# Attention B of a four-layer hybrid kernel: value products stream 128 columns instead of 96, the mask product contracts 128 rows instead of 88

## The chip, the cores and the metric

The kernel runs on one core of one Trainium2 chip, as one launch. The metric is the device time of that core in microseconds (us), the median over runs. Inside the core there are five engines with queues of their own: TensorE (PE for the matmul, PEld for the load of its stationary operand), VectorE (DVE), ScalarE (ACT), GpSimd (POOL) and SyncE (SP, which only issues transfers here). They wait for each other by semaphores.

## The reference, cut to what matters

The input `x` is (32, 256, 128) in f32. Four residual layers follow each other; the third is the one that the change touches:

```python
x = x + attn_a(layernorm(x))
x = x + ffn(layernorm(x))
x = x + attn_b(layernorm(x))
x = x + ffn(layernorm(x))

# attn_b: 16 heads of width 8, T = 256 tokens in 4 segments of 64
for each segment (q, k, v):
    A_mem = (sigma(q) @ M) / (sigma(q) . z + eps)      # memory of the segments before
    scores = where(causal, -inf, q @ k.T / sqrt(8))
    A_dot = softmax(scores) @ v                        # inside the segment
    A = beta * A_mem + (1 - beta) * A_dot
    M, z = M + sigma(k).T @ (v - V_prev), z + sum(sigma(k))
out = A @ W_o.T
```

## The kernel before

The program is three blocks one after the other: `attention_a` (to about 920 us of the trace), `dense` (the second half of attention A's block and the first feed-forward, to about 1150 us), and `attention_b` (from about 1150 us to the end; it also holds the last feed-forward, folded into one matrix for each pair of batch elements).

`attention_b` runs over 32 batch elements as a software pipeline: in step `n`, each engine does the input and projections of element `n`, scores and memory of element `n - 1`, softmax and value products of elements `n - 1` and `n - 2`, and the output of element `n - 3`. A step has `ST = 8` stages `s`, and the order within a stage is written out by hand for each engine. The first steps are peeled, the middle is a loop over pairs of steps. No planner orders anything: each engine executes its list and waits where the list says.

What PE does in each stage, in this order (all in the function for `block.tensor`):

- **The mask product and the transposed scores, L1507 and L1512.** One bf16 matmul puts minus the row maximum and the causal mask into `t_ps` for two heads: its moving operand is `late` (rows 0 to 63: the mask; rows 64 to 87: the row maxima in three bf16 parts for eight heads), its stationary operand is `pick`, which selects from them. Both tiles have `BROWS = 64 + 24 = 88` rows. Eight small products (64 x 64, in pairs) add the scores. ACT takes the exponential into `prob` (L1424).
- **The value product, L1558.** For the two heads of pair `g` (`before(lag, g)` names them) and each half `t` of the tokens, `prob` (128 x 128, f32) is the stationary operand, and `WIN = 96` columns of `vb`, from `at = g * VP` on, stream through. `VP = 36` columns belong to the pair; the columns behind them fall where the next pairs write later, so what they write is overwritten. The profile counts two passes of PE for each f32 matmul: 8 pairs x 2 halves x 2 passes = 32 passes of L1558 for an element, 1024 in all. When all eight pairs are done, DVE normalizes (L1838 to L1842), and PE may start on `o_ps` of the next element only then (`ad_d`).
- Between them stand, at their stages: the scores for the row maxima (L1529, L1533), the recurrence over the segments (L1486, L1493, with DVE between them), the transposes (L1545, L1569, L1572, L1581, L1588, L1623), the projections (L1603, L1604 with 256 columns; L1609, eight passes of 128 columns), the output product (L1595, 128 columns) and the folded feed-forward (L1632, 128 columns).

`VW = VP * 7 + WIN` is the width of `vb`. POOL fills `vb` with zeros once (L1307), writes ones beside the values (L1310), and then writes the values of each element (L1334). DVE fills the rows 64 to 127 of `k_st` and `q_st` with zeros in step 0 (`stack_zeros`, L1642 and L1643), and builds rows 64 to 87 of `pick` there (`picks`, L1649 to L1653); ACT copies the masks into rows 0 to 63 of `pick` and `late` (L1403, L1404) and, for each element and half of the heads, the row maxima into rows 64 to 87 of `late` (L1460).

The lines on which the change turns:

```python
WIN = 96
VW = VP * (H // 2 - 1) + WIN
BROWS = SEG + NPART * H // 2
pick, late = sb("pick", [BROWS, H // 4, 2, SEG], BF16), two("late", [BROWS, T], BF16)
...
pe.matmul(t_ps, pick[:, g % (ST // 2), :, :].rearrange("p a k -> p (a k)"),
          late[g // (ST // 2)][:, :], start=True, stop=True)
...
mm = pe.matmul(o_ps[:, t, at:at + WIN], prob[g % 4][:, t * P:(t + 1) * P],
               vb[st][:, t, at:at + WIN], start=True, stop=True)
```

Of the kernel before, what the change touches and what calls it, by code (L numbers as in the profile page):

```python
# [13 lines left out]
F32 = mybir.dt.float32  # L14
BF16 = mybir.dt.bfloat16
# [4 lines left out]
P = 128  # L20
NB, T = 32, 256
NT = T // P
H, HD, R, QK = 16, 8, 8, 32
# [1057 lines left out]
def attention_b(nc, d):  # L1081

    ctx = ExitStack()
    with ctx:
        sb, sem = memory(nc, ctx, "c")
        SEG = 64
# [2 lines left out]
        MW = HV + H  # L1089
        VP = 2 * 2 * (HD + 1)  # L1090

        WIN = 96
        VW = VP * (H // 2 - 1) + WIN
        BROWS = SEG + NPART * H // 2
        ST = 8
# [5 lines left out]
        w_o = sb("w_o", [P, P])  # L1101
        ident, ident16 = sb("ident", [P, P]), sb("ident16", [P, P], BF16)
        causal = sb("causal", [P, 512], BF16)
        pick, late = sb("pick", [BROWS, H // 4, 2, SEG], BF16), two("late", [BROWS, T], BF16)
        pick8 = sb("pick8", [P, H // 2])
        causal32 = sb("causal32", [P, P + SEG])
        diag = sb("diag", [P, MW])
# [34 lines left out]
        spare, loaded, loaded_late = sem("spare"), sem("loaded"), sem("loaded_late")  # L1142
        const_d, beta_d = sem("const_d"), sem("beta_d")
        mask_d, pick_d = sem("mask_d"), sem("pick_d")
        zeros_d = [sem(f"zeros_d{i}") for i in range(2)]

        x_in, xt_in, wc_in = sem("x_in"), sem("xt_in"), sem("wc_in")

# [240 lines left out]
        @block.scalar  # L1389
        def _(act):  # L1390
            act.wait_ge(loaded, N_LOAD * 16)
            act.copy(ident16[:, :], ident[:, :]).then_inc(mask_d, 1)

            def masks():

                act.wait_ge(loaded_late, N_LATE * 16)
                for k in range(2):
                    ks = slice(k * SEG, (k + 1) * SEG)
                    act.copy(causal[ks, :].rearrange("p (c f) -> p c f", c=H // 2),
                             causal32[ks, ks].unsqueeze(1).broadcast_to([SEG, H // 2, SEG])).then_inc(mask_d, 1)  # L1400
                for k in range(2):
                    act.copy(late[k][0:SEG, :].rearrange("p (c f) -> p c f", c=NS),
                             causal32[0:SEG, P:].unsqueeze(1).broadcast_to([SEG, NS, SEG])).then_inc(mask_d, 1)  # L1403
                act.copy(pick[0:SEG, :, :, :].rearrange("p g a k -> p (g a) k"),  # L1404
                         ident[0:SEG, 0:SEG].unsqueeze(1).broadcast_to([SEG, H // 2, SEG])).then_inc(mask_d, 1)
                act.activation(bexp[:, :], beta[:, 0:1], ACT.Exp, scale=-1.0).then_inc(beta_d, 1)

            def body(j, u):
                n, i = 2 * j + u, u
                for s in range(ST):  # L1410
                    if s == 1 and active(j, u, 1):
                        b = n - 1
                        act.wait_ge(sk_p, b + 1)
                        if later(j, b, 1):
                            act.wait_ge(mem_p, b * 3)
                        act.copy(skn[0:SEG, :, :].rearrange("p s f -> p (s f)"),
                                 ps_c[0:SEG, 0:(NS - 1) * P]).then_inc(sk_d, 1)
                    lag, g = turn(s)
                    if active(j, u, lag):
                        b = n - lag  # L1420
                        act.wait_ge(shifted, b * ST + g + 1)
                        if g >= 4 or later(j, b, 1):
                            act.wait_ge(pv, b * ST + g - 3)
                        act.activation(prob[g % 4][:, :], t_ps, ACT.Exp).then_inc(exped, 1)  # L1424
                    if s == 0 and active(j, u, 3):
                        b = n - 3
                        act.wait_ge(at_p, b + 1)
                        if isinstance(b, int) and b == 0:
                            act.wait_ge(beta_d, 4)
                        if later(j, b, 1):  # L1430
                            act.wait_ge(wo_p, b)
                        act.activation(at_b[:, :], ps_a[:, 0:T], ACT.Copy, scale=beta[:, 3:4]).then_inc(at_d, 1)
                    if s == 0 and active(j, u, 0):
                        act.wait_ge(zt_p, n + 1)
                        act.copy(zt[i][:, :, :, :], ps_b[:, 0:T].rearrange("p (s t) -> p s t", s=NS).unsqueeze(2)
                                 .broadcast_to([P, NS, 2, SEG])).then_inc(zt_d, 1)
                    if s == 1 and active(j, u, 0):
                        act.wait_ge(kq_p, n + 1)
                        act.copy(kq[i][:, 0, :], ps_a[:, 0:T]).then_inc(kq_d, 1)
                        act.mul(kq[i][:, 1, :], ps_a[:, T:2 * T], HD ** -0.5).then_inc(kq_d, 1)  # L1440
                    if s == 3 and active(j, u, 0):
                        act.wait_ge(vs_p, n + 1)
                        if later(j, n, 2):
                            act.wait_ge(mem_p, (n - 1) * 3)
                        else:
                            act.wait_ge(const_d, 9 + 7 * n)
                        act.copy(uv[i][0:SEG, :, 0:HV], ps_b[0:SEG, 0:(NS - 1) * P].rearrange("p (s f) -> p s f", f=P)
                                 ).then_inc(vs_d, 1)
                        if later(j, n, 1):
                            act.wait_ge(v_d, n * VD)  # L1450
                        act.copy(vs[:, :, :].rearrange("p s f -> p (s f)"), ps_b[:, :]).then_inc(vs_d, 1)
                        act.wait_ge(pn_d, (n + 1) * 2)
                        if later(j, n, 1):
                            act.wait_ge(sg_d, n)
                        act.activation(nexp[:, :, :], neg[:, :, :], ACT.Exp).then_inc(nexp_d, 1)
                    for h2 in range(2):
                        if s == MT_AT[h2] and active(j, u, 1):
                            b = n - 1
                            act.wait_ge(mt_p, 2 * b + h2 + 1)
                            act.copy(late[h2][SEG:BROWS, :], mt_ps).then_inc(mt_d, 1)  # L1460
                    if s == 5 and active(j, u, 3):
                        b = n - 3
                        act.wait_ge(z4_p, b + 1)
                        act.copy(z4t[:, :], ps_b[:, 0:T]).then_inc(z4t_d, 1)
                if isinstance(j, int) and n == 0:
                    masks()

            pipeline(act, body, ahead=1)

        @block.tensor  # L1470
        def _(pe):
            pe.wait_ge(loaded, N_LOAD * 16)

            def body(j, u):
                n, i = 2 * j + u, u
# [20 lines left out]
                for s in range(ST):  # L1496
                    lag, g = turn(s)
                    if active(j, u, lag):

                        b, st = n - lag, (i + lag) % 2  # L1500
                        if isinstance(b, int) and b == 0 and g == 0:
                            pe.wait_ge(pick_d, 3)
                        if g % (ST // 2) == 0:
                            pe.wait_ge(mt_d, 2 * b + g // (ST // 2) + 1)
                        if g >= 1 or later(j, b, 1):
                            pe.wait_ge(exped, b * ST + g)
                        pe.matmul(t_ps, pick[:, g % (ST // 2), :, :].rearrange("p a k -> p (a k)"),  # L1507
                                  late[g // (ST // 2)][:, :], start=True, stop=True)
                        for c in range(NS):
                            cs = slice(c * SEG, (c + 1) * SEG)  # L1510
                            for hh in range(2):
                                mm = pe.matmul(t_ps[hh * SEG:(hh + 1) * SEG, cs],  # L1512
                                               k_st[st][:, 2 * g + hh, cs], q_st[st][:, 2 * g + hh, cs],
                                               start=False, stop=True, skip_group_check=True)
                        mm.then_inc(shifted, 1)
# [123 lines left out]
        def _(dve):  # L1639
            def stack_zeros(i):  # L1640

                dve.memset(k_st[i][SEG:P, :, :].bitcast(F32), 0.0).then_inc(zeros_d[i], 1)  # L1642
                dve.memset(q_st[i][SEG:P, :, :].bitcast(F32), 0.0).then_inc(zeros_d[i], 1)  # L1643

            def picks():

                at = lambda a: ident[SEG:BROWS, SEG + a * H // 2:SEG + (a + 1) * H // 2]
                eight = pick8[SEG:BROWS, :]
                dve.tensor_tensor(eight, at(0), at(1), ALU.add).then_inc(pick_d, 1)  # L1649
                dve.wait_ge(pick_d, 1)  # L1650
                dve.tensor_tensor(eight, eight, at(2), ALU.add).then_inc(pick_d, 1)
                dve.wait_ge(pick_d, 2)
                dve.tensor_copy(pick[SEG:BROWS, :, :, :].rearrange("p g a k -> p (g a) k"),  # L1653
                                eight.unsqueeze(2).broadcast_to([BROWS - SEG, H // 2, SEG])).then_inc(pick_d, 1)

# [271 lines left out]
```

## Time and profile before

| | us |
|---|---|
| median of 3 runs | 2051.97 |
| lowest and highest | 2045.56, 2061.51 |
| the profiled execution, its own time | 2052.87 |
| its span in the trace | 2050.7 |
| PE busy | 1686.4 (82%) |
| PEld busy | 1405.3 (69%) |
| DVE busy | 1417.8 (69%) |
| POOL busy | 841.3 (41%) |
| ACT busy | 772.2 (38%) |
| mean granted clock of PE | 0.849 |

The profile is one execution of the program. Busy shares are means over three blocks with different limits, so they say little about one of them. The granted clock is the share of full speed at which PE's array was clocked: it has two levels, 1.00 (2.4 GHz) and 0.50 (1.2 GHz), and a figure between them is a mean over a stretch in which both occurred. The same matmul takes about twice as long at the lower level, and counts as busy all that time. So a stretch that shows more busy time of PE need not hold more work.

### The profile page before, as it was taken

The page shows a single profiled execution, that of the slowest core. Times are in us where ns is not written, and L with a number is a line of the kernel's source. Part 1 is how long each engine was busy: PE and PEld are TensorE (multiplying, and loading weights), DVE is VectorE, ACT ScalarE, POOL GpSimd, SP SyncE. Part 2 cuts the span into 40 slices and gives each one's busy share as a digit, 9 for nine tenths or more (in the row PEclk, how much of TensorE's full clock was granted, in tenths as well). Part 3 has the DMA queues.
Part 4 walks back from the last instruction along what each step waited for, and adds up shares of the span by engine and source line. Part 5 has one row for each costly group of instructions (what it writes and reads, how often), then busy time and mean ns, then how long its engine had stood idle before and what let it go on. Part 6 is the DMA issues. An engine that isn't in the chain of part 4 may idle for free. (4 is left out here: it accounts for less than half of the span.)

```text
span 2050.7 us, 47252 instructions
## 1 busy us (share of the span) xinstructions
PE 1686.4 (82%) x14500; PEld 1405.3 (69%) x14564; DVE 1417.8 (69%) x3490; ACT 772.2 (38%) x1666; POOL 841.3 (41%) x1052
## 2 busy tenths in 40 slices
PE   5999999999999999994666378888888888888887
PEld 3888888888888888893555356666666666666665
DVE  5578888888888888875888555655565555555653
ACT  1455555555555555561222222222222222222221
POOL 3445455444454554534556323333333333323330
PEclk9999999999999999996998667877787777777775
DMA  3322222222211222213332122222222222222220
GB/s 115 122 73 81 74 73 72 74 77 72 72 69 69 72 75 71 75 40 95 96 92 82 55 87 81 88 79 74 73 82 77 80 80 80 76 82 80 77 80 17
DMA packets 178621, 158.10 MB, mean 77 GB/s; under 512 B 9457, under 2 KB 160113, under 8 KB 178546
## 3 DMA queue, kind: packets, MB, share of 16 engines
q1 hardware_dynamic: 178546, 157.16, 23.2%
q8 instruction: 40, 0.66, 0.1%
q14 instruction: 35, 0.29, 0.1%
HBM read 113.09 MB, written 44.04 MB: 77 GB/s over the span
## 5 line engine op out<-in xcount | busy, mean ns | idle before, releaser
L600 PE MATMUL a_bank<-a_vp,a_prob 128*128 128x96 f32 x4096 | 544.5, 277 | 0.3 <-ACT a_prob L457 0.3
L600 PEld LDWEIGHTS a_bank<-a_vp,a_prob 128*128 128x128 f32 x4096 | 511.0, 196 | 17.0 <-ACT a_prob L457 8.7
L633 DVE TENSOR_REDUCE a_nmax<-a_bank 128x2 f32<-128x512 f32 x512 | 331.3, 686 | 122.1 <-PE a_bank L527 121.7
L457 ACT ACTIVATE a_prob<-a_bank 128x512 f32<-128x512 f32 x512 | 306.1, 598 | 179.2 <-PE a_bank L582 170.3
L1558 PE MATMUL c_o_bank<-c_vb,c_prob 128*128 128x96 f32 x1024 | 218.7, 351 | 37.4 <-DVE c_ad L1842 36.4
L1558 PEld LDWEIGHTS c_o_bank<-c_vb,c_prob 128*128 128x128 f32 x1024 | 185.5, 253 | 51.4 <-DVE c_ad L1842 34.6
L527 PE MATMUL a_bank<-a_k_st,a_q_st 96*128 96x256 bf16 x1024 | 206.4, 285 | 8.4 <-DVE a_nmax L633 6.2
L582 PE MATMUL a_bank<-a_q_st,a_k_st 120*128 120x256 bf16 x1024 | 201.8, 279 | 0.0
L1424 ACT ACTIVATE c_prob<-c_bank 128x256 f32<-128x256 f32 x256 | 98.4, 385 | 232.6 <-PE c_bank L1512 229.4
L335 POOL TENSOR_TENSOR a_prod<-a_ov,a_wgt 128x2048 f32<-128x2048 f32 x32 | 119.1, 3721 | 144.5 <-DVE a_wgt L706 131.8
L466 ACT COPY a_ov<-a_bank 128x292 f32<-128x292 f32 x256 | 103.0, 403 | 114.0 <-PE a_bank L600 114.0
L364 POOL TENSOR_SCALAR a_q_st<-a_mt 24x2048 bf16<-24x2048 bf16 x64 | 122.3, 1911 | 39.8 <-PE a_bank L582 23.8
L1352 POOL TENSOR_SCALAR c_parts<-c_kq 128x512 bf16<-128x512 f32 x32 | 19.9, 621 | 282.9 <-ACT c_kq L1440 282.9
L1334 POOL TENSOR_SCALAR c_vb<-c_vs 64x128 f32<-64x128 f32 x128 | 39.8, 311 | 224.0 <-PE c_o_bank L1558 173.6
L735 DVE TENSOR_REDUCE a_ao<-a_prod 128x128 f32<-128x1024 f32 x64 | 126.0, 2011 | 7.7 <-POOL a_prod L335 7.7
L527 PEld LDWEIGHTS a_bank<-a_k_st,a_q_st 96*128 96x128 bf16 x1024 | 102.7, 107 | 32.3 <-DVE a_nmax L633 15.3
L1512 PEld LDWEIGHTS c_bank<-c_q_st,c_k_st 128*64 128x64 bf16 x2048 | 61.2, 126 | 74.0 <-issue 67.1
L582 PEld LDWEIGHTS a_bank<-a_q_st,a_k_st 120*128 120x128 bf16 x1024 | 100.5, 107 | 15.3 <-issue 0.4
L1533 PE MATMUL c_bank<-c_k_st,c_q_st 128*64 128x64 bf16 x2048 | 66.9, 217 | 35.4 <-issue 21.2
L1493 PE MATMUL c_bank<-c_mz,c_sg 128*128 128x144 f32 x192 | 60.4, 404 | 42.1 <-DVE c_mz L1727 42.1
L1711 DVE TENSOR_REDUCE c_nmax<-c_bank 128x8 f32<-128x512 f32 x128 | 85.8, 679 | 10.2 <-PE c_bank L1533 9.9
L1512 PE MATMUL c_bank<-c_q_st,c_k_st 128*64 128x64 bf16 x2048 | 92.0, 220 | 0.0
(198 smaller groups left out, 3073.0 us busy)
## 6 DMA issues: line engine op xcount, KB each, us to landing
a_q_st<-scratch_a_parts_dram SPq DMA_DIRECT2D x192, 96.0 KB
a_k_st<-scratch_a_parts_dram SPq DMA_DIRECT2D x64, 288.0 KB
c_q_st<-scratch_c_parts_dram SPq DMA_DIRECT2D x192, 96.0 KB
c_k_st<-scratch_c_parts_dram SPq DMA_DIRECT2D x64, 288.0 KB
scratch_a_parts_dram<-a_parts SPq DMA_DIRECT2D x32, 384.0 KB, 2.7
scratch_c_parts_dram<-c_parts SPq DMA_DIRECT2D x32, 384.0 KB, 2.7
a_x<-in_x SPq DMA_DIRECT2D x32, 128.0 KB, 10.6
scratch_y<-a_y SPq DMA_DIRECT2D x32, 128.0 KB, 9.3
```

Of the source, the lines that this page charges most:

```text
L335: pool.tensor_tensor(prod[:, :, :].rearrange("p g (r e) -> p g r e", r=R), ov[o][:, :, 0:RD].rearrange("p g (r e) -> p g r e", r=R), wgt[: ...
L364: pool.tensor_scalar(q_st[o][MROW:AROWS, hs, :], mt[half_][MROW:AROWS, :].unsqueeze(1).broadcast_to([AROWS - MROW, H // 2, T]), 1.0, 0.0, ...
L457: act.activation(prob[h % 4][:, :, :].rearrange("p a b -> p (a b)"), t_ps[h % 2][:, :], ACT.Exp).then_inc(exped, 1)
L466: act.copy(ov[(i + lag) % 2][:, 4 * g:4 * g + 4, :], o_ps[g % 2][:, 0:4 * VC].rearrange("p (g c) -> p g c", g=4)[:, :, 0:CQ]).then_inc(ov_ ...
L527: mm = pe.matmul(s_ps[t][:, hh * T:(hh + 1) * T], q_st[o][0:MROW, 2 * g + hh, t * P:(t + 1) * P], k_st[o][0:MROW, 2 * g + hh, :], start=Tr ...
L582: mm = pe.matmul(t_ps[h % 2][:, c * T:(c + 1) * T], k_st[o][0:AROWS, h, c * P:(c + 1) * P], q_st[o][0:AROWS, h, :], start=True, stop=True)
L600: mm = pe.matmul(o_ps[g % 2][:, at:at + VC], prob[h % 4][:, c, t * P:(t + 1) * P], vp[o][:, c, :], start=c == 0, stop=c == NT - 1)
L633: dve.tensor_reduce(nmax[:, t, 2 * g:2 * g + 2], s_ps[t][:, :].rearrange("p (h k) -> p h k", h=2), AX.X, ALU.max, negate=True).then_inc(ma ...
L735: dve.tensor_reduce(ao[o][:, t, :].rearrange("p (h e) -> p h e", h=H), prod[:, :, :].rearrange("p (h i) (r e) -> p i h e r", i=NT, r=R)[:, t],
L1424: act.activation(prob[g % 4][:, :], t_ps, ACT.Exp).then_inc(exped, 1)
L1512: mm = pe.matmul(t_ps[hh * SEG:(hh + 1) * SEG, cs], k_st[st][:, 2 * g + hh, cs], q_st[st][:, 2 * g + hh, cs], start=False, stop=True, skip ...
L1558: mm = pe.matmul(o_ps[:, t, at:at + WIN], prob[g % 4][:, t * P:(t + 1) * P], vb[st][:, t, at:at + WIN], start=True, stop=True)
```

## The change

The value product streams 128 columns of `vb` instead of 96. `vb` grows by 32 columns for each half (`VW` from 348 to 380), which stay zero or hold values of later pairs; the result's extra columns lie in `o_ps` up to column 380 of 512 and are overwritten or not read.

`pick` and `late` get 128 rows instead of 88, and the mask product contracts all of them. Rows 88 to 127 are set to zero once: DVE gets a memset for each of the two `late` tiles (beside the two of `stack_zeros`) and one for `pick`, with a step more in the chain of `pick_d`; ACT waits for the memset of `late` (`late_d`) before its first two copies into it. The number of matmuls, their order, and all other waits stay.

```diff
-        WIN = 96
+        WIN = 128
...
-        pick, late = sb("pick", [BROWS, H // 4, 2, SEG], BF16), two("late", [BROWS, T], BF16)
+        pick, late = sb("pick", [P, H // 4, 2, SEG], BF16), two("late", [P, T], BF16)
...
-        zeros_d = [sem(f"zeros_d{i}") for i in range(2)]
+        zeros_d, late_d = [sem(f"zeros_d{i}") for i in range(2)], sem("late_d")
...
                             b = n - 1
+                            if isinstance(b, int) and b == 0:
+                                act.wait_ge(late_d, h2 + 1)
                             act.wait_ge(mt_p, 2 * b + h2 + 1)
...
-                            pe.wait_ge(pick_d, 3)
+                            pe.wait_ge(pick_d, 4)
...
                 dve.memset(q_st[i][SEG:P, :, :].bitcast(F32), 0.0).then_inc(zeros_d[i], 1)
+                dve.memset(late[i][SEG:P, :].bitcast(F32), 0.0).then_inc(late_d, 1)
...
             def picks():
 
+                dve.memset(pick[SEG:P, :, :, :].rearrange("p g a k -> p (g a k)").bitcast(F32), 0.0
+                           ).then_inc(pick_d, 1)
+                dve.wait_ge(pick_d, 1)
```

## Rows read from the trace of the kernel before

**Rows 1.** The page: span, busy time of each engine, and granted clock by slice.
```profile
span 2050.7 us, 47252 instructions
...
PE 1686.4 (82%) x14500; PEld 1405.3 (69%) x14564; DVE 1417.8 (69%) x3490; ACT 772.2 (38%) x1666; POOL 841.3 (41%) x1052
...
PEclk9999999999999999996998667877787777777775
```

**Rows 2.** Windows, attention A: bounds, length, busy of each engine, PEclk, DMA, GB/s.
```profile
50.00:900.00 850.00, 775.50 (x6440) 706.54 (x6439) 699.79 (x1332) 452.77 (x924) 414.44 (x424) 0.96 0.22 76
```

**Rows 3.** Windows, 24 periods of attention B, L1609 to L1609: some, and the sum.
```profile
1474.51:1501.95 27.44, 22.90 (x219) 17.41 (x220) 15.92 (x52) 7.55 (x19) 8.52 (x15) 0.75 0.22 76
1501.95:1526.43 24.48, 19.89 (x218) 14.91 (x220) 15.40 (x52) 7.51 (x19) 8.77 (x15) 0.86 0.26 86
...
1580.88:1608.99 28.11, 23.69 (x219) 18.17 (x221) 15.98 (x52) 7.54 (x19) 8.52 (x15) 0.70 0.22 75
1608.99:1634.29 25.30, 20.95 (x219) 15.81 (x222) 15.66 (x53) 7.53 (x19) 9.02 (x15) 0.80 0.25 83
...
1740.23:1769.07 28.84, 25.05 (x220) 18.93 (x220) 15.27 (x52) 7.54 (x19) 8.39 (x15) 0.64 0.21 73
...
sum 641.22, PE 533.94 PEld 405.35 DVE 375.29 ACT 180.34 POOL 208.02; mean PE 22.25 PEld 16.89 DVE 15.64 ACT 7.51 POOL 8.67
```

**Rows 4.** Windows around two falls of the clock in attention B.
```profile
1512.30:1515.70 3.40, 1.61 (x18) 1.15 (x17) 3.10 (x13) 0.75 (x2) 1.28 (x4) 0.99 0.31 102
1515.70:1522.50 6.80, 6.33 (x45) 4.46 (x44) 1.49 (x4) 1.78 (x5) 0.00 (x0) 0.50 0.35 121
...
1584.00:1587.40 3.40, 1.58 (x20) 1.08 (x16) 2.66 (x7) 0.54 (x2) 2.57 (x4) 0.99 0.14 31
1587.40:1604.40 17.00, 15.57 (x116) 12.26 (x117) 8.03 (x28) 3.79 (x10) 1.22 (x4) 0.50 0.28 99
```

**Rows 5.** Timeline of PE, clock 0.50: start, us, line, tiles, shapes, count.
```profile
1590.63 1.17 PE L1558 MATMUL c_o_bank<-c_vb,c_prob 128*128 128x96 f32 x4
1591.59 1.11 PE L1632 MATMUL c_bank<-c_wc,c_z4t 128*128 128x128 f32 x4
1592.49 0.42 PE L1507 MATMUL c_bank<-c_late,c_pick 88*128 88x256 bf16 x1
...
1603.36 1.11 PE L1603 MATMUL c_bank<-c_zt,c_w_kq 128*128 128x256 f32 x2
```

**Rows 6.** Timeline of PE, the same two kinds of product at clock 1.00.
```profile
1509.77 0.69 PE L1558 MATMUL c_o_bank<-c_vb,c_prob 128*128 128x96 f32 x4
1510.29 0.64 PE L1632 MATMUL c_bank<-c_wc,c_z4t 128*128 128x128 f32 x4
1510.76 0.27 PE L1507 MATMUL c_bank<-c_late,c_pick 88*128 88x256 bf16 x1
```

**Rows 7.** Single lines over the whole trace: count, duration ns min/median/max, first and last start.
```profile
L1507 PEld LDWEIGHTS c_bank<-c_late,c_pick x256: 95/116/211, 1193.6 to 2032.7; 88*128 88x128 bf16 x128
L1529 PEld LDWEIGHTS c_bank<-c_causal,c_ident x128: 95/98/152, 1181.2 to 2011.9; 128*128 128x128 bf16 x128
```

**Rows 8.** Groups by line and form, 1200 to 2000 us: count, busy, mean ns.
```profile
L1558 PE MATMUL c_o_bank<-c_vb,c_prob 128*128 128x96 f32 x960 | 201.3, 346 | 35.7 <-DVE c_ad L1842 34.7 <-POOL c_vb L1334 1.0
...
L1507 PE MATMUL c_bank<-c_late,c_pick 88*128 88x256 bf16 x240 | 80.6, 336 | 0.0
```

**Rows 9.** Chain that ended last, 1500 to 1560 us: start, us, what.
```profile
1519.82 0.80 PE c_o_bank L1558 x4
1520.62 0.91 PE c_bank L1603 x2
...
1524.15 1.16 POOL c_rest L1353
```

**Rows 10.** Timeline of DVE in the first steps of attention B.
```profile
1161.88 1.76 DVE L1643 MEMSET c_q_st<- 64x2048 f32 x1 [0.37 <-issue]
...
1170.36 0.63 DVE L1680 TENSOR_SCALAR c_z<-c_x,c_mv,c_rs 128x128 f32<-128x128 f32 x2 [4.69 <-POOL c_rs L1321]
...
1183.16 0.31 DVE L1722 TENSOR_TENSOR c_mz<-c_bank,c_diag 128x144 f32<-128x144 f32 x1 [5.52 <-PE c_bank L1486]
```

**Rows 11.** Single line: POOL's memset of `vb`.
```profile
L1307 POOL MEMSET c_vb<- x2: 683/683/683, 1159.4 to 1171.1; 128x696 f32 x2
```

More of the change, by code:

```diff
@@ L1649, in picks @@
                 dve.tensor_tensor(eight, at(0), at(1), ALU.add).then_inc(pick_d, 1)
-                dve.wait_ge(pick_d, 1)
+                dve.wait_ge(pick_d, 2)
                 dve.tensor_tensor(eight, eight, at(2), ALU.add).then_inc(pick_d, 1)
-                dve.wait_ge(pick_d, 2)
+                dve.wait_ge(pick_d, 3)
                 dve.tensor_copy(pick[SEG:BROWS, :, :, :].rearrange("p g a k -> p (g a) k"),
```

## The prediction

> **What bounds the kernel now.** I read the page first. PE is busy 82% of the span, and its clock is near full in the first half and lower in the last [rows 1]. The change touches attention B alone, so I compared the blocks by windows: attention A runs at a mean clock of 0.96 [rows 2], and 24 consecutive periods of attention B (from one start of the value projection L1609 to the next, one batch element each) at 0.76. They sum to 641.22 us, or 26.72 us a period, with PE busy 22.25 us of it [rows 3]. DVE, the next engine, is busy 15.64 us. Attention B is PE's, with parts of each period in which PE waits for others.
>
> Then I looked at the periods one by one, since the same work is done in each. They don't take the same time: 24.48 us at a clock of 0.86, 25.30 at 0.80, 27.44 at 0.75, 28.11 at 0.70, 28.84 at 0.64 [rows 3]. Of the 24, seven lie at 0.86, four at 0.80, three at 0.75 to 0.76, nine at 0.70 and one at 0.64. The number of instructions is equal, and so, within half a microsecond, is what DVE does. So the clock sets the period: from 0.70 to 0.86 is worth 28.11 - 24.48 = 3.63 us. That is the price list for everything below.
>
> Next: what goes before a fall and a rise. Twice the clock fell to 1.2 GHz behind a stretch in which PE was busy less than half the time: 1.61 of 3.40 us, and 1.58 of 3.40 us [rows 4]. That is the place where PE waits for DVE (the recurrence, and the normalization before the next value products: 34.7 us in all behind L1842 [rows 8]). The rise is the odd part. In one period the clock stayed low for 6.8 us, in the next for 17.0 us, though PE was busy 15.57 us of these 17.0, or 92% [rows 4]. So "busy" is not what brings it back. What ran there was value products of 96 columns, mask products of 88 rows and pairs of 64-column products; it rose when the wide projections L1603 and L1604 (256 columns, 128 rows) had run, the first of them at 1603.36, one microsecond before the stretch ended [rows 5].
>
> **The change, part by part.**
>
> *Value products, direct cost.* 1024 passes stream 32 columns more. The trace has both widths side by side. At 1.2 GHz four passes of 96 columns take from 1590.63 to 1591.59, 0.96 us, and the four passes of 128 columns behind them from there to 1592.49, 0.90 us [rows 5]. At 2.4 GHz the same two take 0.52 and 0.47 us [rows 6]. The wider one is not slower in either: every f32 pass loads 128 stationary columns, and this load, which both have, sets the pace. I take 0. Bounds: none below 0; above, if the pass were paced by its columns, the pitch of 0.130 us would grow by a third, 0.043 us, at 2.4 GHz (0.240 and 0.080 at 1.2 GHz), which is 1024 x 0.043 = 44 us to 1024 x 0.080 = 82 us. The rows stand against that.
>
> The Trainium skill ("TensorE: Matmul & The Clock Gate", section "Back-to-back issue gap") has a rule that speaks against the change: the gap between matmuls is the streamed columns over the clock plus a small constant. By it 32 columns more are an estimated 13.3 ns a pass at 2.4 GHz, or 14 us for 1024 passes, and the sum below would come out 14 us higher. This trace does not agree: four passes of 128 columns take no longer than four of 96, 0.47 against 0.52 us.
>
> *Value products, tail.* The result of the last pass comes up to 32 columns later, once an element where DVE waits for it; a fourth of a pass's 0.130 to 0.240 us is 0.03 to 0.06, times 32 elements 1 to 2 us at most. I take 0 and leave 2 us in the range.
>
> *Mask product.* 256 products contract 40 rows more. Its load of 88 rows takes at least 95 ns, that of the causal product with 128 rows at least 95 ns as well, medians 116 and 98 [rows 7]: rows cost nothing. I take 0. If the busy time of 336 ns a product [rows 8] grew as the rows do, by 45%, it would be 256 x 0.15 = 39 us; nothing in the rows points there.
>
> *Start.* The memset of 64 x 2048 f32 takes 1.76 us [rows 10]. The two of `late` (64 x 128) and the one of `pick` (64 x 256) are a sixteenth and an eighth of it, 0.11 and 0.22 us, say 0.3 each with their starts, 0.9 us in all. The first `late` and all behind it in DVE's queue come ahead of waits of 4.69 us for POOL and of 5.52 us for PE [rows 10], which hide them; if the cover were gone it would be 0.9 us once. POOL's memset of `vb` grows from 696 to 760 columns, 683 ns by a tenth, twice [rows 11]: 0.1 us. ACT's two new waits are for memsets long past when its first copies come; nothing queues behind them. Value 0, bounds 0 and 1 us.
>
> *The clock.* What is left is whether fuller products bring the clock back sooner. Every stage has one group of four value passes and one mask product. The value passes put a third more columns through the array without taking longer, and the mask product uses all 128 rows instead of 88. In the 17.0 us stretch that is nearly all of what ran between the narrow score products. The fall behind the idle gap stays: the change puts no work into it. So no period should do better than those that already fall and recover fast, 24.48 us at 0.86. The lower bound of the effect is none: each period as it is.
>
> Between them I choose by the periods. The eleven at 0.80 or above have short low stretches and I leave them. The thirteen at 0.76 or below sum to 365.3 us, 28.10 each; they hold stretches like that of 17.0 us, busy and low, and these I let come down to the 25.30 us of a period at 0.80. That is 13 x (28.10 - 25.30) = 36.4 us over 24 periods, 1.52 us each; attention B has 31 periods between its 32 elements, so 31 x 1.52 = 47 us. It lies on the path: in the low stretch the chain of waits goes through the value products and projections one behind the other, and then through POOL's split, which the clock doesn't shorten [rows 9]; the period rows have this in them already, since they are whole periods.
>
> **The sum.** 0 + 0 + 0 - 47 = -47 us against the profiled execution's 2052.87 us (span 2050.7 and 2.2 around it): 2005.9. The median of the runs lies 0.9 lower, at 2051.97, so I forecast 2005.
>
> **The rivals.**
>
> 1. *The clock doesn't follow the width.* For it: attention A uses value products of the same 96 columns and holds 0.96 [rows 2]; its PE is busy 775.5 of 850 us, and maybe gaps alone decide. Against it: 15.57 busy us of 17.0 at 1.2 GHz [rows 4]. The time is then that of before, 2052 (with the start, 2053).
>    The Trainium skill (same page, section "Why this matters for your kernels") advises keeping TensorE busy without long idle gaps, and names no width. By that rule this change does nothing to the clock, as in this rival. The trace agrees for the falls, which stand behind gaps, and not for the 17.0 us.
> 2. *All periods recover at once.* Every period goes to 24.48: 31 x (26.72 - 24.48) = 69 us, so 1983. For it: all periods hold the same work, and only thirteen of 24 are in the long form. Against it: even the short ones split, seven at 0.86 and four at 0.80, so a mixture is what equal work settles in. If the falls went too, the same price of 3.63 us for 0.16 would give 0.14 x 22.7 = 3.2 us a period more and 1884; PE's waits for DVE are not touched, so I give it almost nothing.
> 3. *Slower: the extra columns set the pace.* Place: the 1024 passes of L1558. The load and the stream may be balanced such that 128 columns fit only where the neighbours are of the same kind. Price 0.043 to 0.080 us a pass, 44 to 82 us; without a gain of the clock 2096 or more. It decides from 47 / 1024 = 0.046 us a pass on: there it eats the forecast gain. Against it: [rows 5, 6].
>
> **How the numbers follow.** Forecast (half to most of the long low stretches go, 1990 to 2030): 0.47. Rival 2 and better (below 1990): 0.20. Rival 1, with a gain too small to see (2032 to 2056): 0.27. Rival 3: 0.06. The range reaches from a little below rival 2, 1972, to just past the kernel as it is, 2054; it holds about 0.85, and the likeliest case's own range is 1990 to 2030. One per cent, 20.5 us, is about what a measurement of this kernel can tell from no change (its three runs spread over 16 us). Faster by over 1%, below 2031: 0.67. Within 1%: 0.27. Slower: 0.06.
>
> **What would show it.** In the changed kernel's profile: the mean clock of attention B's periods near 0.82 instead of 0.76; periods at 0.70 with 28 us rare, those at 0.80 and 0.86 with 24.5 to 25.3 us common; four passes of L1558 still 0.5 us apart at 2.4 GHz and 0.9 to 1.0 at 1.2; L1507 at 88 and 128 rows alike; attention A unchanged at 0.96. Rival 1 is shown by an equal split of period lengths, rival 3 by a pitch of L1558 at 2.4 GHz of 0.17 us. The forecast is wrong if the clock stays low through busy stretches of full-width products, or if the periods grow shorter by less than the price list says because POOL's or DVE's part of the chain takes over.

## The result and the profile after

The changed kernel takes 1995.56 us (median of 4 runs, 1986.52 to 2002.17) against 2048.76 us of the kernel before (4 runs, 2042.15 to 2061.51): 53 us less, ratio 0.973 with a 95% interval of 0.9666 to 0.9794. The profiled execution is the shortest of its four (1986.52 us), so its trace shows somewhat more gain than the medians do: spans of 2050.7 and 1984.6 us, 66 us apart. Below, times of whole kernels are medians, and times of parts come from the traces. Two runs of the variants below, one with 64 columns (2160.99 us) and one with less than half of the added work (1955.85 us), fell in a slower state of the chip and are left out of the medians.

The page of the changed kernel, against [rows 1]: span, busy time of each engine, and granted clock by slice of the span.

```profile
span 1984.6 us, 47321 instructions
...
PE 1630.1 (82%) x14564; PEld 1344.4 (68%) x14564; DVE 1418.8 (71%) x3493; ACT 771.1 (39%) x1666; POOL 839.4 (42%) x1052
...
PEclk9999999999999999997898968988888888888887
```

DVE, ACT and POOL are as busy as before to within 2 us. PE streams more columns and is busy 56 us less. The clock row has mostly 8 where it had 7 in attention B; ahead of it the mean clock is the same in both traces, 0.96 from 50 to 900 us and 0.85 from 900 to 1150 us.

Windows of the changed kernel: 24 consecutive periods of attention B, then two of them, to be held against [rows 3] (columns: bounds, length, busy time of PE, PEld, DVE, ACT, POOL with counts, granted clock, DMA share, GB/s).

```profile
1299.98:1899.74 599.76, 499.62 (x5280) 365.23 (x5281) 376.51 (x1225) 179.71 (x456) 206.92 (x337) 0.85 0.25 84
...
1521.93:1547.94 26.01, 22.12 (x220) 15.95 (x220) 15.47 (x52) 7.50 (x19) 8.70 (x15) 0.80 0.24 81
...
1649.96:1673.65 23.69, 19.19 (x220) 14.34 (x220) 15.94 (x52) 7.40 (x19) 8.53 (x15) 0.93 0.26 89
```

The sum is 599.76 us where it was 641.22: 24.99 us a period in place of 26.72, at a mean clock of 0.85 in place of 0.76. Of the 24 periods, 13 lie at 0.86, seven at 0.80 and four at 0.93. Not one is at 0.76 or below, where thirteen were. The price list still holds: 24.3 to 25.1 us at 0.86 (24.4 to 25.2 before), 25.8 to 26.0 at 0.80 (25.3 to 26.2 before), 23.7 at 0.93.

The falls themselves stayed. Counted in the two traces over the 24 periods, the clock falls to 1.2 GHz 37 times before and 39 times after. What changed is how long it stays there: 303.8 us in all before, 174.1 after. Before, twelve of the stretches at 1.2 GHz lasted 10 to 20 us; after, none lasts more than 6.8 us, and 27 of the 39 are over after 3.4 us, like this one of the period at 0.93:

```profile
1656.46:1659.88 3.42, 3.42 (x35) 2.81 (x34) 2.42 (x9) 0.65 (x3) 0.00 (x0) 0.50 0.18 75
```

Where the 66 us of the two spans come from: 2.7 us ahead of the first period (start of the first L1609 at 1162.6 and of the same product, now L1611, at 1159.9 us), 52 us in the 31 periods, and 11 us behind the last of them, which the next rows show, before and after:

```profile
1978.97:2050.70 71.73, 56.25 (x440) 42.96 (x441) 29.54 (x100) 13.62 (x34) 9.59 (x18) 0.55 0.12 38
```

```profile
1924.10:1984.60 60.50, 44.04 (x441) 32.65 (x441) 29.59 (x101) 13.56 (x34) 9.98 (x18) 0.77 0.14 45
```

The pipeline drains there with the same 440 matmuls, at a clock of 0.55 before and 0.77 after. Part of these 11 us may be chance: the trace of the kernel that differs from the one before in attention A alone (128 columns there, below) has the same drain at a clock of 0.71, in 63.4 us.

A fall of the clock in the changed kernel, as in [rows 4]: PE waits (3.04 us busy of 4.80), the clock falls, and it rises again after 6.8 us.

```profile
1682.60:1687.40 4.80, 3.04 (x34) 2.24 (x33) 3.99 (x16) 1.13 (x3) 1.25 (x4) 0.98 0.29 95
1687.40:1694.20 6.80, 6.80 (x46) 4.66 (x44) 1.49 (x4) 1.69 (x4) 0.00 (x0) 0.51 0.35 119
```

### The profile page after: what moved, and what is told of

Its sections match the earlier page's. It is cut to its first block and busy times, and to the rows that moved or that the text cites. A ratio compares the mean times of both kernels' runs of the same rounds, so it can differ in the third digit from the quotient of the medians.

```text
span 1984.6 us, 47321 instructions
## 1 busy us (share of the span) xinstructions
PE 1630.1 (82%) x14564; PEld 1344.4 (68%) x14564; DVE 1418.8 (71%) x3493; ACT 771.1 (39%) x1666; POOL 839.4 (42%) x1052
## 5 line engine op out<-in xcount | busy, mean ns | idle before, releaser
L1560 PE MATMUL c_o_bank<-c_vb,c_prob 128*128 128x128 f32 x1024 | 198.5, 323 | 39.3 <-DVE c_ad L1848 39.3
L1560 PEld LDWEIGHTS c_o_bank<-c_vb,c_prob 128*128 128x128 f32 x1024 | 158.8, 220 | 52.2 <-DVE c_ad L1848 35.0
L1514 PEld LDWEIGHTS c_bank<-c_q_st,c_k_st 128*64 128x64 bf16 x2048 | 56.5, 118 | 64.0 <-issue 56.2
L1495 PE MATMUL c_bank<-c_mz,c_sg 128*128 128x144 f32 x192 | 50.0, 342 | 44.5 <-DVE c_mz L1733 44.5
L1514 PE MATMUL c_bank<-c_q_st,c_k_st 128*64 128x64 bf16 x2048 | 86.2, 210 | 0.0
L1509 PE MATMUL c_bank<-c_late,c_pick 128*128 128x256 bf16 x256 | 78.8, 308 | 0.0
```

The source lines that it names most:

```text
L1514: mm = pe.matmul(t_ps[hh * SEG:(hh + 1) * SEG, cs], k_st[st][:, 2 * g + hh, cs], q_st[st][:, 2 * g + hh, cs], start=False, stop=True, skip ...
```

## The experiments

Theory W: the wider value products bring the clock back sooner, and do nothing else. Its rivals: the 128 rows of the mask product do it; the wider products help PE by themselves; it is chance in how the periods meet the falls. Beside it theory F: the falls come from the gaps in which PE waits for DVE.

### Each half alone

128 columns, 88 rows:

```diff
-        WIN = 96
+        WIN = 128
```

> The value products stream 128 columns, the mask product keeps 88 rows. Theory W (the columns of the value products bring the clock back sooner): most of the change's gain of 53 us is here, 35 to 50 us off the kernel before, mean clock of attention B's periods 0.83 to 0.86 against 0.76. Rival R (it is the 128 rows of the mask product): within 10 us of the kernel before, clock 0.76 to 0.78. Rival S (the phase in which the clock's falls meet the periods shifted, by chance): anything between, and not in step with the width.

Measured: 1996.91 us, ratio to before 0.973 (0.9657 to 0.9804). The whole gain, within 2 us of the full change, and 3 us more than the 50 that I had expected at most. Its 24 periods:

```profile
1310.24:1911.06 600.82, 500.89 (x5280) 366.41 (x5281) 375.60 (x1225) 179.77 (x456) 206.85 (x337) 0.85 0.25 84
```

96 columns, 128 rows (the changed kernel with one line back):

```diff
-        WIN = 128
+        WIN = 96
```

> The mask product contracts 128 rows, the value products keep 96 columns. Theory W: 0 to 18 us faster than before, since these are 8 matmuls of about 45 in each period and gain 40 rows of 128. Rival R: 35 to 53 us faster. If both e1 and this one give the whole gain, either is enough to cross what the clock wants; if neither does, it needs both.

Measured: 2024.42 us (2007.01 to 2032.29), ratio 0.9826 (0.9737 to 0.9916). Faster than the kernel before by more than the expected 18 us: 26 us by the medians, 36 by the ratio of runs. The periods:

```profile
1318.01:1942.56 624.55, 533.41 (x5281) 394.75 (x5281) 372.43 (x1225) 180.18 (x456) 207.79 (x337) 0.79 0.24 81
```

They are 0.70 us shorter each. All 31 periods of this trace, which is of the slowest of its four runs, are 18 us shorter than those before (798.4 and 816.4 us), just within what I had expected. So rows count too, though how much is less certain than for the columns; the two halves don't add: 53 and 26 us alone, 53 together. The columns are sufficient, and on top of them the rows bring nothing that can be measured.

### The width as a dose

The kernel before with fewer columns, and the changed kernel with more:

```diff
-        WIN = 96
+        WIN = 64
```

> The kernel before with 64 columns in place of 96. Theory W, other direction: the clock stays low longer, mean 0.65 to 0.72 in attention B, 20 to 60 us slower than before although less is streamed. Rival C (streamed columns cost time and nothing else): not slower; each group of four passes ends 32 columns earlier, 27 to 53 ns, so up to 10 us faster.

```diff
-        WIN = 128
+        WIN = 160
```

> The changed kernel with 160 columns in place of 128. Up to 128 columns the load of the weights paces a pass (112 ns at 2.4 GHz, 213 at 1.2 in both traces); beyond it the columns do: 32 more are 64 cycles a pass, 27 to 53 ns, 1024 passes, 28 to 55 us of PE time. Theory W: the clock rises further, to 0.88 to 0.92 in attention B, which gives back 10 to 25 us; sum 5 to 30 us slower than the changed kernel. If the pace were still the load's, it would be 10 to 25 us faster than the changed kernel.

```diff
-        WIN = 128
+        WIN = 192
```

> The changed kernel with 192 columns. With 160 the pitch of a pass was 136 ns at 2.4 GHz and 267 at 1.2 (the columns pace it), and still the clock (0.91 in attention B) gave back more than that cost. 192 should take 160 and 320 ns a pass, 1024 x 24 = 25 us more at 2.4 GHz. Theory W: the clock can gain at most 0.09 more, worth 10 to 20 us at 2 us a period for 0.09, so 0 to 20 us slower than with 160 columns; the best width is near 160. If each further column paid for itself, it would be faster than 1980.

| columns | median, us | ratio to before (95%) | clock of the 24 periods | their mean length, us |
|---|---|---|---|---|
| 64 (88 rows) | 2132.72 | 1.0366 (1.0265 to 1.0466) | 0.56 | 29.51 |
| 96 (before, 88 rows) | 2050.15 | 1 | 0.76 | 26.72 |
| 128 (88 rows) | 1996.91 | 0.973 (0.9657 to 0.9804) | 0.85 | 25.03 |
| 160 (128 rows) | 1979.91 | 0.963 (0.9558 to 0.9703) | 0.91 | 24.42 |
| 192 (128 rows) | 1979.15 | 0.9658 (0.96 to 0.9716) | 0.92 | 24.57 |

The clock follows the width over the whole range, so it isn't chance. (Between 128 and 160 the rows change too; at 128 columns they brought nothing that could be measured.) With 64 columns, less work, the kernel is 83 us slower, at a clock of 0.56; I had expected at most 60, and 0.65 to 0.72. Its 24 periods, and a stretch of 42 us in them:

```profile
1319.78:2028.05 708.27, 671.35 (x5280) 497.50 (x5281) 359.09 (x1232) 181.00 (x456) 206.18 (x339) 0.56 0.21 71
...
1480.00:1522.00 42.00, 40.12 (x295) 29.58 (x294) 20.19 (x70) 10.38 (x26) 9.70 (x18) 0.50 0.23 76
```

PE is busy 40.12 of 42.00 us and its clock stays at 1.2 GHz throughout. The longest such stretch, from 1647.07 us to the end of the trace, lasts 483.53 us, with PE busy 459.04 us of it. So busy time alone does not bring the clock back; between these kernels only the width of the products differs.

The low stretches of the 24 periods tell how the width acts. From 96 to 128 columns the falls stay and the stretches shorten (37 falls with 304 us at 1.2 GHz, then 39 with 174 us). With 160 columns there are 25 falls and 109 us, with 192 there are 17 and 89 us: here some falls are gone too, although PE waits for DVE as before (with 160 columns 37.0 us in 24 waits ahead of L1495 and 28.9 in 24 ahead of L1560, against 35.0 and 28.6). That is more than theory W said.

I had expected 160 columns to lose 5 to 30 us against 128. They won 16. The cost is there as foreseen; the single lines of the value product, with 128 and then 160 columns (durations in ns, minimum, median, maximum):

```profile
L1560 PE MATMUL c_o_bank<-c_vb,c_prob x1024: 272/275/582, 1194.9 to 1970.6; 128*128 128x128 f32 x171
```

```profile
L1560 PE MATMUL c_o_bank<-c_vb,c_prob x1024: 299/299/636, 1203.4 to 1967.8; 128*128 128x160 f32 x171
```

With 192 columns the minimum is 325 ns and the median 326. Each 32 columns more are 24 to 27 ns a pass at 2.4 GHz, 25 us of PE's time for 1024 passes. The gain of the clock from 0.85 to 0.91 is worth more: by the price of 22.7 us for a clock of 1, an estimated 0.06 x 22.7 = 1.4 us a period, 42 us over 31. That is on the high side. The run of 160 columns with the clock held up, below, puts the cost on the path at 16 us; with the 16 us that were won, the clock gave back about 32. From 160 to 192 columns the medians are equal and the periods 0.15 us longer: gain and cost cancel within what the runs can tell.

### The clock held up by other means

The decisive test takes the clock away from the change. Where PE waits for DVE, it gets bf16 products of 512 columns to do, whose result nobody reads: 5 ahead of the second L1493, 2 ahead of the transposes L1545 and 4 ahead of an element's first value products.

```diff
+                def fill(lag, count):
+
+                    if active(j, u, lag) and later(j, n - lag, 1):
+                        if lag == 1:
+                            pe.wait_ge(maxed, (n - 1) * NU + 2)
+                        for _ in range(count):
+                            pe.matmul(s_ps[1][:, :], ident16[:, :], causal[:, :], start=True, stop=True)
...
                     if s == 4 and active(j, u, 1):
+                        fill(1, 5)
                         recalled(1)
                     if s == 0 and active(j, u, 0):
+                        fill(2, 2)
                         pe.wait_ge(z_d, (n + 1) * NT)
...
+                        if g == 0:
+                            fill(2, 4)
                         pe.wait_ge(exped, b * ST + g + 1)
```

On the kernel before (96 columns, 88 rows):

> The kernel before (96 columns, 88 rows) with work added where PE waits for DVE: in each period 5 bf16 products of 512 columns ahead of the second L1493, 2 ahead of L1545, 4 ahead of the first value products of an element (11 x 0.213 = 2.3 us at 2.4 GHz, against about 3 us of waiting there); they write a score bank that is free, and nothing reads them. Theory F (the falls come from the idle gaps): the clock of attention B goes from 0.76 to 0.95 or more, periods of 22 to 23 us, 90 to 130 us faster than before. If the clock stays under 0.85, the gaps are not what makes it fall; if it is at 1.0 and the time falls by less than 60 us, the added work is not hidden.

On the changed kernel (128 and 128):

> The changed kernel (128 columns, 128 rows) with the same added work. The pair with the run before is the test of the cause. Theory W (the change acts through the clock alone, and by itself costs 26 ns a group of four passes where a bf16 load follows, about 3 us): with the clock held up in both, the change's 53 us shrink to within 10 us of zero or turn into a small loss. A rival in which the wider products help PE by themselves: again about 50 us faster than its partner.

On 160 columns and 128 rows:

> 160 columns, 128 rows, and the same added work. With the clock held up, the 24 ns a pass (136 against 112) are a loss that nothing gives back: 1024 x 24 = 25 us slower than the run before at most, 10 to 25 us, although without the added work 160 columns were 16 us faster than 128. If it is again faster than 128 columns, width does something beyond the clock.

On 64 columns and 88 rows:

> 64 columns, 88 rows, with the added work in the waits. Without the added work 64 columns were 82 us slower than 96. Theory W with F: if the added work holds the clock at 1.00 here too, that loss is gone and the time is 1895 to 1910, as with 96 and 128 columns (each group of four passes may end 27 ns earlier, up to 3 us). If the gaps' filling is not enough at 64 columns, the clock falls and the time is well over 1910; width then matters even without gaps.

| columns, rows | without added work, us | with it, us | ratio to before (95%) |
|---|---|---|---|
| 64, 88 | 2132.72 | 1910.44 (1906.91 to 1916.67) | 0.9308 (0.9265 to 0.9351) |
| 96, 88 | 2050.95 | 1906.55 (1900.48 to 1916.32) | 0.9309 (0.926 to 0.9358) |
| 128, 128 | 1995.56 | 1905.22 (1904.61 to 1906.89) | 0.9289 (0.9249 to 0.9329) |
| 160, 128 | 1979.91 | 1921.15 (1917.73 to 1929.72) | 0.9374 (0.9326 to 0.9422) |

Windows of the 24 periods with the added work, 96 columns first, then 128:

```profile
1293.67:1821.39 527.72, 473.36 (x5473) 336.74 (x5545) 374.89 (x1225) 177.70 (x456) 207.80 (x337) 1.00 0.28 95
```

```profile
1295.91:1824.42 528.51, 474.68 (x5472) 337.33 (x5545) 374.86 (x1225) 177.66 (x456) 207.14 (x337) 1.00 0.28 95
```

With 160 columns the same 24 periods take 541.11 us, with 64 columns 527.25. The clock is 1.00 in all four. The 53 us of the change are then 1.3 us by the medians, with overlapping runs, and the periods of the two kernels are 21.99 and 22.02 us. The 83 us that 64 columns lost are 4 us, and the 16 us that 160 columns had won over 128 are now 16 us lost. So the change acts through the clock: shown, by taking the clock away from it in both directions. The 16 us that 160 columns cost here show also that a longer value product would still be seen with the added work in place. And work in the gaps takes the falls away: PE executes 11 products more in each period, none of the 37 falls is left, and the kernel before becomes 144 us faster, 14 more than the upper end of what I had written down. That it must be the gaps that are filled is not shown: the same products at another place of the period were not tried, and with 160 and 192 columns some falls went although the gaps stayed.

The waits of PE in the 24 periods show that the added work stands in the gaps: the kernel before, then the same with the added work (columns: who waited for whom, us in total, times, longest).

```profile
PE c_bank L1493 <- DVE c_mz L1727: 35.0, 24, 1.8
PE c_o_bank L1558 <- DVE c_ad L1842: 28.6, 24, 1.4
```

```profile
PE c_o_bank L1570 <- DVE c_ad L1854: 8.8, 24, 0.5
...
PE c_bank L1493 <- DVE c_mz L1739: 7.8, 12, 0.7
```

### Less than half of the added work

```diff
-                        fill(1, 5)
+                        fill(1, 2)
...
-                        fill(2, 2)
+                        fill(2, 1)
...
-                            fill(2, 4)
+                            fill(2, 2)
```

> The kernel before with less than half of the added work: 2, 1 and 2 products in the same three places (1.1 us a period in place of 2.3). If only the complete closing of a gap counts, this gives little, under 40 us. If it counts how much runs in the stretch, as the widths say, it gives 60 us or more, and the clock lies between 0.85 and 1.00.

Measured: 1926.71 us (1922.53 to 1932.64), ratio 0.9392 (0.9342 to 0.9442), clock 0.97:

```profile
1304.24:1844.54 540.30, 453.02 (x5329) 335.46 (x5401) 375.34 (x1225) 177.74 (x456) 207.54 (x337) 0.97 0.28 93
```

21 of the 24 periods are at 1.00, and three falls are left. Five products of 0.21 us in a period bring 128 us by the medians (2055.19 us before, measured beside it) where eleven brought 144; by the ratios it is 125 of 142. The gaps need not be closed for most of the gain.

### Attention A

```diff
-VC = 96
+VC = 128
```

> The kernel before with the same widening in attention A alone (value products stream 128 columns in place of 96, 4096 passes). Its clock is 0.96 there already. Price: a group of eight passes is always followed by a bf16 load, so the 26 ns found in attention B apply to nearly all of 512 groups, 13 us. Gain: low time in attention A is 8% of 850 us; if half of it goes, about 10 us. Sum -12 to +13 us against before, likeliest no change that can be measured; a gain like attention B's would say that the share of low time is not what limits it.

Measured: 2035.16 us (10 runs), ratio 0.9924 (0.9887 to 0.9961), so 0.4 to 1.1% faster. I had thought no change the likeliest, and 12 us the most: the ratio gives 16, the medians 20. The clock of attention A, against [rows 2]:

```profile
50.00:900.00 850.00, 777.84 (x6541) 700.05 (x6540) 712.12 (x1358) 460.92 (x937) 415.88 (x425) 0.99 0.22 76
```

Its last value product starts at 913.1 us in place of 922.4. Of the 18 falls in this window two are left, and the time at 1.2 GHz is 24 us in place of 75; I had let half of it go. At half speed 51 us less are worth an estimated 25 us of PE's time, against 13 us for 26 ns a group. The trace has about as much gain again, 8 us, in the drain at the end, which the edit doesn't touch.

### Both together

The kernel before, with the added work in attention B and 128 columns in attention A:

> The two that helped for different blocks together: attention B with 96 columns and 88 rows as before and the added work in its waits (1906.6 us alone, clock 1.00 in its periods), and attention A with 128 columns (0.76% or 15 us off alone, its clock 0.99 against 0.96). The blocks run one after the other, so theory W says the gains add: 1888 to 1898 us. If they don't add, something that the two share (not the blocks' own clocks) made one of them.

Measured: 1897.11 us (6 runs, 1891.28 to 1903.11), ratio 0.9261 (0.9226 to 0.9296). It is the fastest here, 7.4% under the kernel before and 98 us under the changed one. Of attention A's 16 us (0.76%) 9 are seen by the medians; the runs of this kernel spread over 12 us, so the 7 that lack say nothing.

## Why the prediction was right, and where it was not

**The forecast** was 2005 us in a range of 1972 to 2054, measured 1995.56: 53 us off where 47 were forecast, by the mechanism that was forecast.

**What bounds the kernel: right.** The price list from the periods carried the sum. From 0.76 to 0.85 its 22.7 us for a clock of 1 give 2.0 us a period; the rows say 1.73. Its premise of equal periods was a little loose: DVE's busy time ranges over 0.9 us in the 24 periods, more than I wrote, and those at 0.86 take either 24.4 to 24.7 us or 25.1 to 25.2.

**Direct cost of the columns: the value near right, the reading wrong.** I took "four passes of 96 columns 0.52 us, four of 128 behind them 0.47" [rows 6] to show that the wider ones are no slower. The same two groups in the changed kernel:

```profile
1681.47 0.71 PE L1560 MATMUL c_o_bank<-c_vb,c_prob 128*128 128x128 f32 x4
1682.02 0.61 PE L1634 MATMUL c_bank<-c_wc,c_z4t 128*128 128x128 f32 x4
1682.47 0.27 PE L1509 MATMUL c_bank<-c_late,c_pick 128*128 128x256 bf16 x1
```

0.55 and 0.45 us: the sum of both groups is 1.00 us (0.99 before), but 26 ns by the finer starts have moved from the second to the first. Behind a narrow group the next stream starts early. The gain is given back where a long f32 load follows (186 to 192 ns at 2.4 GHz; with the clock held up, the product behind L1632 starts 995 ns after the value products with 64, 96 and 128 columns alike) and kept where a shorter load does: the bf16 ones (L1507, L1623) and the transposes of L1569 (about 140 ns). Ahead of L1507, behind an L1493, the four passes take 0.42 us before and 0.44 after (0.80 and 0.85 at 1.2 GHz). Three of eight groups in an element are of that sort: 96 groups of 26 to 53 ns, 3 to 5 us if nothing hid them. With the clock held up, the periods differ by 0.03 us, 1 us in all. I had put 0 for it, and had read the two groups as if the width could not show. Inside a group it doesn't: from pass to pass it is 112 ns at 2.4 GHz with 64, 96 and 128 columns alike, which fits the load that all three share, and then 136 ns with 160 and 163 with 192. (My 130 ns a pass were a quarter of the time to the next group.)

The rule of the Trainium skill that I weighed ("TensorE: Matmul & The Clock Gate", section "Back-to-back issue gap") gives the gap of isolated matmuls, which grows with the streamed columns, and says that in a stream of loads and matmuls both set the spacing. Taken for each of 1024 passes, its estimated 13.3 ns for 32 columns would be 14 us. These runs don't agree up to 128 columns, where only the last pass of a group shows the width; from 128 on a slope is there, 24 to 27 ns for 32 columns of these f32 passes, twice the 13.3.

**Mask product and start: right.** Its load takes at least 95 ns with 128 rows too, median 100 where it was 116 at 88 [rows 7]. The memsets took 0.17 us each for `late` and 0.27 for `pick`, 0.6 in all; the waits behind them on DVE were 4.53 and 5.20 us in place of 4.69 and 5.52 [rows 10]. What I had not priced apart is that the mask product's rows move the clock as well, 26 us by themselves.

**The clock: right in kind, a little short in size.** I let thirteen periods come down to 25.30 us and left eleven. In the trace all thirteen are gone, and the mean is 24.99, not 25.20. That the falls stay since their gaps stay was right too, 39 against 37. The step that failed is "no period should do better than those that already fall and recover fast, 24.48 us at 0.86": four are at 0.93 with 23.7 us. The period of 24.48 us has one stretch of 6.8 us at 1.2 GHz, and I took it for the least that can be. With the wider products 27 of the 39 stretches are over after 3.4 us, and a period with only one of these is at 0.93; before, four of 37 were that short. The second omission is the drain behind the last period, at a clock of 0.55, up to 11 us in the traces: I counted only the 31 periods. That 53 us came out so near 47 owes something to luck: the profiled runs differ by 66 us, and the runs of one kernel spread over 16 to 19 us.

**The rivals.** Rival 1, the clock doesn't follow the width: refuted by the dose, 0.56 to 0.92 from 64 to 192 columns. Its argument, that attention A holds 0.96 with 96 columns, was true and proved nothing: A falls more rarely (18 times in 850 us, PE busy 91% of them), and with 128 columns it went to 0.99. The rule of the Trainium skill that I cited with it ("TensorE: Matmul & The Clock Gate", section "Why this matters for your kernels"), to keep TensorE busy, is half of the truth here: work in the gaps was worth 144 us, but a PE busy 40.12 of 42.00 us stayed at 1.2 GHz. Rival 2, every period at 0.86 at once, 1983 us: the mean clock got there, by a mixture of 0.80 to 0.93; the time lies between it and the forecast. Rival 3, the columns set the pace: wrong at 128, where a pass takes 112 ns as with 64 and 96, and right at 160 and 192, where each 32 columns cost 25 us of PE's time (16 us of the kernel's at 160, with the clock held up) and the clock more than paid for the first 32 only.

**What stays open.** What exactly brings the clock back, columns, rows or the part of the array that is in use, can't be told from these runs: both halves move it, and they don't add. That the clock rose once when the wide projections L1603 and L1604 had run [rows 5] proves nothing about them: with 64 columns they ran in every period, and in 16 of the 24 the clock did not rise at all. Whether products at another place than the gaps would hold the clock as well was not tried. Why the mask product's rows alone bring 26 to 36 us, with a spread of its runs of 25 us, is not settled either. `dense`, whose clock is 0.82 to 0.85, and the last 60 us were not tried.

## What to carry to other kernels

If the same loop body takes different times in different periods, list length against granted clock: that gives the price of the clock without any model (it came out somewhat high here, 2.0 us a period for 1.73), and says whether it is worth working on. Then look first at what PE does in its waits: a few matmuls that nobody needs, placed ahead of a wait, brought 144 us here where the widening brought 53, and made the widening pointless. Where gaps can't be filled, f32 products with 128 stationary columns can be padded to 128 streamed columns at almost no cost: a pass took 112 ns with 64, 96 and 128; and the test for "it acts through the clock" is to hold the clock up by other means and see the effect vanish.

## What the runs showed of the hardware that was not expected

- A PE that was busy 96% of 42 us stayed at 1.2 GHz throughout when its value products streamed 64 columns, and then for the last 483 us of the trace, 95% busy.
- With 128 columns in place of 96 the clock fell as often (39 and 37 times in 24 periods) and came back sooner (174 and 304 us at 1.2 GHz).
- Streaming fewer columns made the kernel slower: 64 in place of 96, 83 us. Going from 128 to 160, where each pass takes 24 ns longer, made it 16 us faster still.
- Five bf16 products of 512 columns in a period of about 26 us, 1.1 us of work, took the mean clock from 0.76 to 0.97.
- Up to 128 columns, the time from a group of f32 passes to the product after next says nothing of its width where a load of 186 to 192 ns follows (995 ns across L1632 with 64, 96 and 128 columns): what the narrow group gains is paid back in the next. The width shows only ahead of a shorter load.
